# The last 64 features of a shared down projection: high and low halves stacked on 128 rows

## What is computed

```python
shared = jax.nn.silu(x @ Ws_gate) * (x @ Ws_up) @ Ws_down      # inner width 704
scores = jax.nn.softmax(x @ W_router, axis=-1)
topk_vals, topk_idx = jax.lax.top_k(scores, TOP_K)             # 2 of 8 experts
...
h = jax.nn.silu(jnp.einsum('td,edh->eth', xf, We_gate)) * jnp.einsum('td,edh->eth', xf, We_up)
y_all = jnp.einsum('eth,ehd->etd', h, We_down)                 # inner width 352
routed = jnp.einsum('etd,te->td', y_all, combine)
return routed.reshape(b, s, d) + shared
```

## Time and profile before

| | |
|---|---|
| three runs | 1499.71, 1501.74, 1508.71 us; median 1501.74 |
| profiled execution | 1504.44 us, of it the span of the trace 1502.7 us |
| PE matmuls | 1449.3 us busy, 96% of the span, 8274 instructions |
| PE weight loads | 1255.6 us, 84% |
| DVE | 1049.4 us, 70% |
| POOL | 791.6 us, 53% |
| ACT | 784.6 us, 52% |
| DMA | 222.15 MB, mean 148 GB/s |
| granted TensorE clock, mean | 0.986 of full speed |

### The profile page before, as it was taken

The page is one execution under the profiler, slowest core; times in us unless marked ns, Lnnn a source line. Parts: engine busy times, 40 slices in busy tenths (PEclk is TensorE's granted clock), DMA queues, the critical chain, the costliest instruction groups (busy, mean ns, idle before and its releaser), DMA issues. The chain is left out here.

```text
span 1502.7 us, 22382 instructions
## 1 busy us (share of the span) xinstructions
PE 1449.3 (96%) x8274; PEld 1255.6 (84%) x8274; DVE 1049.4 (70%) x1750; ACT 784.6 (52%) x1343; POOL 791.6 (53%) x480
## 2 busy tenths in 40 slices
PE   6999999999999999999999999999999999999999
PEld 5878999989987687788778779778878999999887
DVE  7584665677557898688769878867665665677466
ACT  3313666666532467565656656654215666666511
POOL 3203777777545345645643654662016777677543
PEclk9999999999999999998999999999999999999999
DMA  8232877877554120020012011016044877787444
GB/s 313 85 116 87 284 271 255 276 271 269 205 185 118 62 84 1 29 71 29 1 58 69 1 43 57 1 39 225 30 136 147 300 264 255 278 275 275 148 131 168
DMA packets 79739, 222.15 MB, mean 148 GB/s; under 512 B 8400, under 2 KB 16592, under 8 KB 78224
## 3 DMA queue, kind: packets, MB, share of 16 engines
q1 hardware_dynamic: 57552, 163.04, 30.9%
q0 software_dynamic: 11360, 37.23, 8.3%
q10 hardware_dynamic: 10720, 20.45, 3.8%
HBM read 183.47 MB, written 37.22 MB: 147 GB/s over the span
## 5 line engine op out<-in xcount | busy, mean ns | idle before, releaser
L665 POOL TENSOR_TENSOR g_lo<-g_raw,g_hi 128x1408 fp32r<-128x1408 f32 x54 | 180.7, 3345 | 113.7 <-ACT g_hi L830 111.4
L665 POOL TENSOR_TENSOR u_lo<-u_raw,u_hi 128x1408 fp32r<-128x1408 f32 x54 | 174.6, 3233 | 59.1 <-ACT u_hi L830 59.1
L1865 PE MATMUL bank<-u_hi,xgT 128*128 128x352 f32 x624 | 168.5, 333 | 0.0
L1888 PE MATMUL bank<-d_hi,hT 128*128 128x512 f32 (+1 forms) x468 | 159.3, 394 | 5.4 <-DVE hT L1170 5.4
L1865 PE MATMUL bank<-g_hi,xgT 128*128 128x352 f32 x624 | 163.0, 323 | 0.0
L695 POOL DMA_INDIRECT xg<-token_x,row_of x78 | 88.0, 1128 | 137.8 <-DVE row_of L1315 121.4
L880 ACT ACTIVATE gate<-bank 128x512 f32<-128x512 f32 (+1 forms) x48 | 28.7, 598 | 221.0 <-PE bank L1818 220.2
L751 POOL TENSOR_TENSOR w_hl<-w_raw,w_hl 128x1024 fp32r<-128x1024 f32 x35 | 89.4, 2553 | 94.2 <-ACT w_hl L830 94.2
L1833 PE MATMUL bank<-d_hi,hT 128*128 128x512 f32 (+1 forms) x384 | 127.1, 403 | 4.5 <-DVE hT L1170 2.4
L1170 DVE TENSOR_TENSOR d_lo<-d_raw,d_hi 96x512 fp32r<-96x512 f32 (+2 forms) x54 | 121.5, 2250 | 0.0
L1520 DVE SCALAR_TENSOR_TENSOR acc<-pre,cw,acc 128x512 f32<-128x512 f32 x120 | 114.7, 956 | 4.3
(11 more groups left out here) (264 smaller groups left out, 3667.6 us busy)
## 6 DMA issues: line engine op xcount, KB each, us to landing
g_raw<-in_w_gate SPq DMA_DIRECT2D x54, 704.0 KB, 6.1
u_raw<-in_w_up SPq DMA_DIRECT2D x54, 704.0 KB, 6.7
d_raw<-in_w_down SPq DMA_DIRECT2D x46, 512.0 KB, 5.0
w_raw<-in_w_in SPq DMA_DIRECT2D x36, 512.0 KB, 3.5
routed_y<-ys ACTq DMA_DIRECT2D x32, 512.0 KB, 4.6
d_raw<-in_w_down SPq DMA_DIRECT2D x46, 192.0 KB, 5.3
token_x<-xn SPq DMA_DIRECT2D x8, 1024.0 KB, 6.3
X<-in_x SPq DMA_DIRECT2D x4, 1024.0 KB, 10.0
```

What stands on the lines that cost most here:

```text
L665: pool.tensor_tensor(half_of(piece, 1, s), raw_at[piece][s % RING][:], half_of(piece, 0, s).bitcast(F), ALU.subtract)\
L1865: ins = pe.matmul(dst[:, 0:FE], xgT[:, n % 2, hx, kc], half_of(piece, hw, NS + j)[:, kc], start=(m == 0), stop=(m == 3 * KD - 1))
L1888: ins = pe.matmul(bank[Y + n % 2][:], hT[0:fw, hh, c, 0:P], half_of(2, hw, NS + j)[0:fw, c], start=(m == 0), stop=(m == 3 * NF - 1))
```

## The change

For the block `MIXED` the low half of the hidden features is written into rows 64 to 127 of the high half's tile, `hT[64:128, 0, 2]`, under the high half in rows 0 to 63. The 64 rows of down weights are put twice into the input, one after the other (`w_down_shared` gets 64 more rows), so that the third block of the second set has 128 rows like all others of the shared sets. Two matmuls of 128 rows then form high x high + low x high and high x low + low x low. The three of 64 rows go. All matmuls of `down` now use whole tiles.

```diff
     def last_rows(s):
 
-        return FE - 2 * P if shared_set(s) is None else SH_W[shared_set(s)][-1]
+        return FE - 2 * P if shared_set(s) is None else P
...
                     dve.wait_ge(f_hhi, v + 1)
-                    lo_half(hT[0:fw, 1, c, 0:width], gate[0:fw, par, 0:width], hT[0:fw, 0, c, 0:width], f_hlo)
+                    lo = hT[fw:P, 0, c, 0:width] if (s, c) == MIXED else hT[0:fw, 1, c, 0:width]
+                    lo_half(lo, gate[0:fw, par, 0:width], hT[0:fw, 0, c, 0:width], f_hlo)
...
                 def down(job, c, s, tiles, free, signal):
 
-                    fw = SH_W[(job - j0) // 2 % NS][c]
+                    terms = [(0, 0), (0, 1)] if ((job - j0) // 2 % NS, c) == MIXED else HALVES
                     pe.wait_ge(f_hlo, job * NF + (c + 1) + LO0)
                     for a in tiles:
                         if c == 0:
                             free(a)
-                        for m, (hh, hw) in enumerate(HALVES):
-                            ins = pe.matmul(bank[4 + a][:], hT[0:fw, hh, c, a * P:(a + 1) * P], half_of(2, hw, s)[0:fw, c],
-                                            start=(c == 0 and m == 0), stop=(c == NF - 1 and m == 2))
+                        for m, (hh, hw) in enumerate(terms):
+                            ins = pe.matmul(bank[4 + a][:], hT[:, hh, c, a * P:(a + 1) * P], half_of(2, hw, s)[:, c],
+                                            start=(c == 0 and m == 0), stop=(c == NF - 1 and m == len(terms) - 1))
...
-        "w_down_shared": a["L0_ffn_Ws_down"],
+        "w_down_shared": np.concatenate([a["L0_ffn_Ws_down"], a["L0_ffn_Ws_down"][-SH_W[MIXED[0]][MIXED[1]]:]]),
```

## The result

The changed kernel takes 1495.04 us (median of 9 runs, 1489.04 to 1498.58), the kernel before, run beside it, 1502.26 us (9 runs, 1499.71 to 1509.15). The ratio is 0.9945, 95% interval 0.9925 to 0.9964: 0.55% faster, and inside the forecast range. The profiled execution took 1498.43 us. One run of all those reported, of the kernel best_wo, had a mean granted clock of 0.846 and took 1592.8 us; it is left out of that kernel's ratio.

What follows compares the result with a forecast made beforehand. The prediction took PE's back-to-back matmuls, 96% of the span, as the bound. Savings at eight places, 4.08 + 1.90 + 1.14 + 0.83 + 0.43 = 8.4 us, 0.56%, took the median from 1501.74 to 1493.4 us, range 1489 to 1499.5.

Steps and rivals of the forecast that it cites:

- steps 1 and 2: At the eight places one of three matmuls and both 128/64-row borders go: 1.36 us at P1, 0.91 matmuls, 0.45 borders and pace.
- P1, P5 and P7: Second-set jobs: job 2 before routed tiles in each FFN phase, job 2 after them in the second; 1.36 us saved each.
- 3 and 4: Third block's wider weight load, 128 to 256 KB, issued well ahead, and its splits on ACT and VectorE: both cost nothing.
- 5: Low half of hidden features written from rows 0 to 63 into rows 64 to 127 on VectorE: taken as costing nothing.
- rival D: Low half written across rows is slow: at 3.70 us the gain is gone, 1501; 1 us more, 1506 to 1507; chance 0.05.
- P8: Job 3 after the routed tiles, second FFN phase, the kernel's end: 0.43 us saved, bound by VectorE's four additions.
- P3: Job 2 after the routed tiles, first FFN phase: 1.14 us saved, the way in hidden by a 0.80 wait.
- P4: Job 3 after the routed tiles, first FFN phase, into the mixer: 0.83 us saved, 0.5 waiting for GpSimd's second low half.
- P2, P6: Job 3 before the routed tiles in each FFN phase: 0.95 us saved each, new wait on VectorE's additions into X.
- Rival C: Waits behind P2, P3, P4 and P6 take more, only P1, P5, P7 and P8 pay: 4.5 us or less, 1497 to 1501; chance 0.13.
- Rival A: The forecast itself, matmuls and borders both come back: 1493.4 us, its own range 1490 to 1497; chance 0.65.
- Rival B: Borders don't come back, the 0.35 us holes belonging to something other than row count: 6.8 us saved, 1494.9; chance 0.12.

Runs made afterwards that it cites:

- best_wo: Changed kernel with dve_order's and pool_order's edits, last down projection tile by tile, large late store cut into four, and wo_late's move; ratio to before 0.9922.
- count_only: Kernel before with the third of the three 64-row matmuls left out, both borders staying; 1496.68 us, ratio to before 0.9946.
- borders_only: Changed kernel with three 128-row matmuls in place of two in the last block, so no matmul is saved; 1501.43 us, ratio to before 0.9982.
- the repetition: Changed kernel run once more with no edit, for a second trace; 1496.91 us, ratio to before 0.9949.
- dve_order: Changed kernel with VectorE's low half of the first routed tile's down weights made behind the four additions into X; 1498.19 us (one run).
- wo_late: Changed kernel with VectorE's two low halves of the output weights made behind the fifth and seventh convolution block in the first turn's mixer; 1493.06 us (one run).
- pool_order: Changed kernel with GpSimd's second low half of the mixer's weights made between the two splits of the output weights; 1498.41 us (one run).

## Why the prediction was right, and where its steps were wrong

The total came out (forecast 1493.4, measured 1495.04), but two of eight places are not as forecast, and their two errors have the same sign. That the ratio, 0.55% for a forecast of 0.56%, fits so closely is luck: count_only, which saves 1.1 to 1.4 us less by its places, measured 0.9946. What the prediction earned is the sign, the range and six of the eight places.

- **Matmuls and borders** (steps 1 and 2): right to 0.04 us at P1, P5 and P7 (1.34 to 1.40 for 1.36). Count and borders were then taken apart by count_only and borders_only: 0.86 to 0.91 and 0.40 to 0.47, for 0.91 and 0.45.
- **Load and splits** (3 and 4): nothing seen. No wait on the down weights appeared or grew on PE. In the trace of before the low half of the last block of down weights takes 0.67 to 0.69 us on 64, 96 and 128 rows alike, and 3.70 to 3.72 each time a split of `g_lo` on GpSimd runs beside it (28 of 54).
- **Low half written across rows** (5): the write lasts 0.69 us instead of 0.68, so rival D is out. The instruction behind it pays, however. From the write's start to the start of the next DVE instruction are 0.61 us before (1493.49 to 1494.10) and in count_only (1486.74 to 1487.35), and 0.71 to 0.72 in the changed kernel, the repetition and borders_only (1495.32 to 1496.04). Before the change the pair is

```profile
1493.49 0.68 DVE L1170 TENSOR_TENSOR hT<-gate,hT 64x512 fp32r<-64x512 f32 x1 [0.70 <-ACT hT L830]
1494.10 1.59 DVE L1357 SCALAR_TENSOR_TENSOR X<-yg,r_val,X 128x512 f32<-128x512 f32 x2
```

and the pair after it stands in the rows of P8 above. So the instruction behind the write starts about 0.10 us later when the write goes to rows 64 to 127; at P3 too it does, 0.60 us behind before (477.81 to 478.41) and 0.72 after (475.52 to 476.24). Why it is held no run shows. The prediction took nothing for it. It costs nothing at P3 (1.15 for 1.14) and 0.1 at P4, where PE's wait for DVE is 2.07 us before, 2.06 in count_only and 2.17 with the changed write, and 0.1 at P8. The table has both: 0.01 in count_only, about -0.1 in the repetition and in borders_only.
- **P2, P6**: forecast 0.95 each with a new wait of about 0.4, measured 0.90 and a bracket of 0.23, which is a start 0.40 late. The cap is the chain named, and dve_order shows it: 0.38 comes back at each.
- **P3**: 1.14 forecast, 1.15 measured, the wait 0.80 became 0.81.
- **P4**: the wrong step. The prediction took the first wait behind the place (0.5 on GpSimd's second low half; 0.37 measured) for the whole cost and wrote down 0.83. The bound lies further on: DVE is 95% busy for the next 40 us, and its order decides when PE's next units can start (wo_late). Every us that PE wins here is waited away by the fourth unit. Worth 0.0 from that start on and, with the held instruction ahead of it, -0.1. The fall of the clock in the changed kernel's trace cost little for the same reason: 27.89 us from P4 to the fourth unit instead of 27.65.
- **P8**: the second wrong step. The sum followed DVE's additions, which are 0.44 us sooner against P7, and not the store queue behind them, whose start hangs on the routed additions. Forecast 0.43, measured -0.1.
- **Sum**: 8.4 less 0.9 at P4, 0.5 at P8 and 0.05 in the rest is 6.9, which would be 0.46% and 1494.9 from the median of 1501.74. The traces give 6.6 and 6.9 at the places.
- **Rival C** (the waits take more) had the right mechanism at one place and the wrong ones besides: P2, P3 and P6 lost no more than 0.05 beyond the forecast. **Rival A**, the forecast itself, had the mechanism, with a term too large in two places. **Rival B**'s time, 1494.9, is nearest to the measured 1495.04, but its mechanism is out by borders_only; the time alone could not have told A from B.

## What to carry to other kernels

Two row-starved products of one sum can share a matmul: where a block of 64 rows is multiplied as high and low halves, stacking the halves on 128 rows with the weights twice makes two matmuls of three and takes the borders between row counts away as well (together 1.34 to 1.40 us a place here, where nothing behind it was late). Price each such place by its own trace, and follow the gain past the first new wait until the shift is steady, over the whole next stage if another engine is nearly always busy there, as DVE was with 95% behind P4. At the end of a kernel look at the queue of stores before the arithmetic: here the last small stores stood behind the large one issued ahead of them, and from the last addition to the end it took 3.2 us, with the large one split 2.5.

## What the runs showed of the hardware

- A change of the stationary operand from 128 to 64 rows and back costs about 0.2 and 0.2 us of PE and a hole of 0.35 in the weight loads at each. A change between 128 and 96 rows costs nothing: in the kernel before, the weight loads of the routed down projection (line 1888) keep their distance of 0.23 us over both borders, with no hole:

```profile
152.08 0.41 PEld L1888 LDWEIGHTS bank<-d_hi,hT 128*128 128x128 f32 x2
152.53 0.19 PEld L1888 LDWEIGHTS bank<-d_lo,hT 96*128 96x128 f32 x1
152.76 0.19 PEld L1888 LDWEIGHTS bank<-d_hi,hT 96*128 96x128 f32 x1
153.00 0.19 PEld L1865 LDWEIGHTS bank<-g_hi,xgT 128*128 128x128 f32 x1
```

- The spread of the runs goes with the granted clock. In ten runs of the repetition the span was 1500.4 at a mean of 0.981 and 1490.6 to 1492.2 at 0.988, some 9 us for 0.007, or 1.3 per 0.001. By arithmetic 0.001 of the mean over 1500 us is 3.0 us at a granted clock of 0.50, in which half the work, 1.5 us, is lost (the pitch there was 0.43 us for 0.227). So a difference of 2 us between kernels sinks in it, while the shift from place to place repeats to 0.04 us where the clock does not fall. Where the stretches fall changes from run to run: the fall at P4 was there in two (changed and pool_order) of the ten traces of kernels whose matmuls at P4 all have 128 rows, each time behind the wait of 2.16 to 2.17 us, which the others had too.
